# ScalarE fetches a second column of each step's fourth row pixel by pixel

## The chip, the core and the metric

The kernel runs on one core of one Trainium2 chip. A core has TensorE (PE; PEld is its weight load), VectorE (DVE), ScalarE (ACT), GpSimd (POOL) and SyncE (SP), each with a queue of instructions that it works through in order, and 16 DMA engines. SP, ACT and POOL can issue DMAs; "SPq" and "ACTq" in a row mark such an issue. Engines wait for one another through semaphores only. The metric is the device time of one execution in microseconds; of several runs the median counts.

## The reference

x is 4 images of 128 x 128 pixels with 64 channels. Four residual blocks are applied in turn, each on a group-normalised x:

```python
x = x + L0(gn(x))   # 3x3 convolution, then 1x1
x = x + L1(gn(x))   # deformable: 2 groups x 9 taps, each sampled at its own place
x = x + L2(gn(x))   # focal modulation: depthwise filters of 3, 5, 7 taps, Gelu, gates
x = x + L3(gn(x))   # triangle product per channel, layernorms, sigmoid gates
# L1, for each pixel, group and tap: place = grid + tap + offset, clipped to the image
out = wa * v[y0, x0] + wb * v[y1, x0] + wc * v[y0, x1] + wd * v[y1, x1]
```

L1 is what matters here: 18 columns (2 groups x 9 taps) of bilinear samples for each pixel, at places that the data decide. After it come a depthwise 3 x 3 and a 1 x 1 convolution.

## The kernel before

**Layout.** Two rows of an image lie side by side on the 128 partitions (64 channels each). For L1 a table in HBM (`table[b]`) holds, for each pixel of image b and each group, an entry with its four neighbours' channels, so one sample is one read of 512 bytes (128 floats).

**Steps.** L1 is computed in 128 steps, 32 for each image; a step does 4 rows (`ROWS`) of 128 pixels, row r into its own buffer `gat[r]`, which has 18 columns of 128 floats for each pixel (a pixel is a partition). For each row:
- POOL gathers a column for all 128 pixels with one indirect DMA (L573): 18 columns a row, but 17 in the fourth row (`gathered_by_pool`, L516), so 71 gathers a step. It waits for the row's indices (`idx_given`) and until the buffer has been summed in the step before (`summed`).
- The missing column (`FETCHED`, the fourth row's last) is fetched by SP, pixel by pixel (`fetch`, L785). SP waits for the places (`pixels_given`), brings them from a column over partitions (`pixel_at`) into one partition (`pixel_row`) with a DMA (L792), waits for that and for the buffer, and then, 16 pixels (`CHUNK`) at a time, loads the places into registers (L799) and issues 16 DMAs of 512 bytes (L804).
- DVE (`row`, L1731) waits for the gathers of the row (and of the fourth row also for the pixels), gives the next indices, multiplies the row by its bilinear weights (L1743) and sums four neighbours into `srow` (L1750). At the start of a step `indices` (L1677) computes places, weights and indices of the next step; its last part writes `pixel_at` once the DMA that reads the places before has landed (L1712).
- PE transposes `srow` into `pt` (L1354, L1358); ACT copies `pt` to `stt` in two copies a row: the first (L1068) and the second (L1072); PE multiplies by the folded weights (L1367) behind each copy.

**What is woven in.** The work of the other blocks stands in stages: for image 0's steps the first block and the tables of the images to come (`AHEAD`), for image b's steps the blocks L2 and L3 of image b - 1 (`BEHIND`): a norm step, 2 of context, 8 of depthwise, 4 of modulate, a norm step, 4 of operands, 2 of triangle, 4 of close, the rest plain, with nothing woven in. The work of the last image follows the 128 steps. For each engine the order is written out by hand: a step spans the times 0 to 14, each flow yields the time of its next piece, and `merged` and `weave` put the pieces in order of these times into the engine's one queue. A row's copies on ACT have the times 3r + 2 and 3r + 3. Between stages SP, ACT, PE and DVE meet (drain and wait for one another); POOL doesn't. In a depthwise step ACT issues the loads of context and bands at time 0 (L522, L526), and Gelu for the filters of 3, 5 and 7 taps (L955) stands at about 3.2, 6.5 and 9.7, each behind PE's filter (L1223). Ln and Exp of the layernorms are issued by `roots` (L966).

Of the kernel before, what the change touches and what calls it, by code (L numbers as in the profile page):

```python
# [23 lines left out]
I32 = mybir.dt.int32  # L24
# [5 lines left out]
ds = bass.ds  # L30
# [18 lines left out]
STEPS = NB * PER  # L49
FETCHED = (3, GK - 1)  # L50
CHUNK = 16
# [152 lines left out]
def build(nc, x, mats, vecs, conv_kt, conv_w, off_w, dw_w, pw_w, dw_b, gate_w, base_loc, base_idx, taps,  # L204
          out):
    ctx = ExitStack()
    with ctx:
        def sb(name, shape, dt=F32):
            return ctx.enter_context(nc.sbuf_tensor(name, shape, dt))
# [4 lines left out]
        def sems(*names):  # L214
            return tuple(ctx.enter_context(nc.semaphore(n)) for n in names)
# [54 lines left out]
        idx = sb("idx", [P, ROWS, GK], U32)  # L270
        pixel_at = sb("pixel_at", [P, 1], I32)
        pixel_row = sb("pixel_row", [1, P], I32)
        wtn = sb("wtn", [P, ROWS, GK, 4])
# [94 lines left out]
        with nc.Block() as block:  # L368
# [82 lines left out]
        turned_full, full_ready = sems("turned_full", "full_ready")  # L451
        pixels_given, pixel_row_in, pixels_in = composed, x_in[1], x_in[2]
        GIVEN0, ROW0, PIXELS0 = 2, 16, 16
        (padded_c,) = sems("padded_c")
# [10 lines left out]

        q_p, q_s, m_p, xo_s, m_cen_p, m_sq_s, m_var_p, m_lg_s, m_rs_s, m_y_s, m_o_p, m_added = sems(
            "q_p", "q_s", "m_p", "xo_s", "m_cen_p", "m_sq_s", "m_var_p", "m_lg_s", "m_rs_s", "m_y_s",
            "m_o_p", "m_added")
        ca_in = sems(*(f"ca_in{u}" for u in range(4)))

        t_cen_p, t_sq_s, t_var_p, t_lg_s, t_rs_s, t_y_s, ab_p, g_p, ab_s, g_s = sems(
            "t_cen_p", "t_sq_s", "t_var_p", "t_lg_s", "t_rs_s", "t_y_s", "ab_p", "g_p", "ab_s", "g_s")
        abg_out = sems(*(f"abg_out{u}" for u in range(4)))
# [3 lines left out]

        c_cen_p, c_sq_s, c_var_p, c_lg_s, c_rs_s, c_y_s, c_o_p, lin_s, res_s = sems(
            "c_cen_p", "c_sq_s", "c_var_p", "c_lg_s", "c_rs_s", "c_y_s", "c_o_p", "lin_s", "res_s")
        s_in, g_in, res_out = (sems(*(f"{n}{u}" for u in range(4))) for n in ("s_in", "g_in", "res_out"))  # L480
# [35 lines left out]
        def gathered_by_pool(r):  # L516

            return GK - 1 if r == FETCHED[0] else GK

# [19 lines left out]
        with nc.Block() as block:  # L539

            @block.gpsimd
            def _(pool):

                def shift_upper(t):
                    nc.gpsimd.tensor_scalar(xn[C:P, 4 * t + 1:4 * t + 5, 1:W + 1],
                                            xb[C:P, t * TILE:(t + 1) * TILE].rearrange("p (h w) -> p h w", w=W),
                                            gn[C:P, 0:1], gn[C:P, 1:2], ALU.mult, ALU.add).then_inc(upper, 1)

                pool.wait_ge(gn_done, 1)
                pool.wait_ge(padded, 1)  # L550
                for t in range(TB):
                    shift_upper(t)
                pool.wait_ge(upper, TB)
                for m in range(MCH):
                    for dy in range(3):
                        for dx in range(3):
                            nc.gpsimd.tensor_scalar(wk[:, m, dx, (3 - dy) * C:(4 - dy) * C], pw[:, m, 0:C],
                                                    dw[:, m, 3 * dy + dx:3 * dy + dx + 1], None, ALU.mult)\
                                .then_inc(wk_ready, 1)
                pool.wait_ge(wk_ready, N_ZERO + MCH * K9)  # L560
                pool.wait_ge(gn_done, 2)
                for t in range(TB):
                    shift_upper(t)
                pool.wait_ge(upper, 2 * TB)

                def step(n, b):
                    for r in range(ROWS):
                        v = n * ROWS + r
                        pool.wait_ge(idx_given, v + 1)  # L569
                        pool.wait_ge(summed, v + 1)  # L570
                        pool.sem_inc(started, 1)  # L571
                        for k in range(gathered_by_pool(r)):
# [11 lines left out]
            def _(sp):  # L584
# [200 lines left out]
                def fetch(n, b, at):  # L785

                    r, k = FETCHED
                    slot = k % K9 * G + k // K9
                    source = table[b].bitcast(U8)
                    yield at  # L790
                    sp.wait_ge(pixels_given, GIVEN0 + n + 1)
                    sp.dma_start(pixel_row[:], pixel_at[:]).then_inc(pixel_row_in, 16)  # L792
                    sp.wait_ge(pixel_row_in, ROW0 + 16 * n + 16)
                    sp.sem_inc(started, 1)
                    sp.wait_ge(summed, ROWS * n + r + 1)
                    sp.sem_inc(started, 1)
                    for first in range(0, P, CHUNK):
                        yield at + 4 * first / P
                        _, starts = nc.values_load_multi_w_load_instructions(  # L799
                            pixel_row[:, first:first + CHUNK], engines=[mybir.EngineType.SP], min_val=0,  # L800
                            max_val=4 * PAIR * (G * TABLE - 1),
                            skip_runtime_bounds_check_because="the coordinates are clipped to the image")
                        for p, start in enumerate(starts, first):
                            sp.dma_start(gat[r][p:p + 1, slot, :].bitcast(U8), source[ds(start, 4 * ENTRY)].unsqueeze(0))\  # L804
                                .then_inc(pixels_in, 16)

# [40 lines left out]
            def _(act):  # L847
# [117 lines left out]

                def roots(n, count, eps_, var_p, lg_s, y_s, rs_s):  # L966

                    for u in range(count + 1):
                        if u < count:
                            act.wait_ge(var_p, n(u) + 1 + count)  # L970
                            nc.scalar.activation(lg[u], banks[2 * u + 1], ACT.Ln, bias=eps_).then_inc(lg_s, 1)
                        if u:
                            act.wait_ge(lg_s, n(u - 1) + 1)
                            act.wait_ge(y_s, n(u - 1) + 1)
                            nc.scalar.activation(rs[u - 1], lg[u - 1], ACT.Exp, scale=-0.5).then_inc(rs_s, 1)
# [5 lines left out]
                def modulate(b, i):  # L981
# [11 lines left out]
                    yield 5  # L993
                    roots(n, flight(b), eps[:, 1:2], m_var_p, m_lg_s, m_y_s, m_rs_s)

                def operands(b, i):
# [7 lines left out]
                    ln_and_exp(b)  # L1004
                    roots(n, flight(b), eps[:, 0:1], t_var_p, t_lg_s, t_y_s, t_rs_s)
                    yield 7
# [29 lines left out]
                def close(b, i):  # L1036
# [12 lines left out]
                    yield 5  # L1049
                    roots(n, flight(b), eps[:, 0:1], c_var_p, c_lg_s, c_y_s, c_rs_s)  # L1050
                    yield 10
# [9 lines left out]
                def step(n, b, i):  # L1061

                    for r in range(ROWS):
# [12 lines left out]
                for a in (*gelu_s, ab_s, g_s, gate_s):  # L1076
                    act.sem_inc(a, 1)
                act.sem_inc(right_entries, 2)
                drive(act, meet, step, lambda: None, {"depthwise": depthwise_begin, "modulate": ln_and_exp, "close": ln_and_exp},
                      {"conv_norm": norm, "shift": shift, "conv_shift": lower_part, "table_norm": norm,  # L1080
# [348 lines left out]
            def _(dve):  # L1429
# [247 lines left out]
                def indices(n):  # L1677
# [27 lines left out]
                    for cx, wx in enumerate((w_lo, w_hi)):  # L1705
# [210 lines left out]
```

## Time and profile before

| | |
|---|---|
| median of 3 runs | 12193.87 us (12193.84 to 12196.55) |
| the profiled execution | 12192.18 us, its span 12190.4 us |
| granted TensorE clock, mean over the span | 0.776 |
| busy: POOL, PE, DVE, ACT | 71%, 63%, 42%, 15% |
| POOL's gathers | 9088 |
| SP's pixel DMAs | 16384 |

Times of a timeline count from the start of the span. "x128" behind a row means that 128 instructions of the kind follow each other; the number after the start is then the time from the first to the last. In square brackets stands how long the engine was idle before and what ended that.

### The profile page before, as it was taken

How to read it: one execution, taken by the hardware profiler on the slowest of the kernel's cores; microseconds unless marked ns; L12 is line 12 of the kernel's file. 1: busy time of each engine (PE TensorE's matmuls, PEld its weight loads, DVE VectorE, ACT ScalarE, POOL GpSimd, SP SyncE). 2: the span in 40 equal slices, each digit the busy share in tenths (PEclk: the TensorE clock that was granted, in tenths of full speed). 3: DMA queues.
4: the chain of work that ended last, by engine and by line, in shares of the span. 5: the costliest groups of instructions: out<-in, count | busy, mean ns of one | idle time of the engine just before them, and what ended most of it. 6: DMA issues, size and time to landing. Idle time of an engine off the chain costs nothing.

```text
span 12190.4 us, 137030 instructions
## 1 busy us (share of the span) xinstructions
PE 7646.7 (63%) x30934; PEld 5412.4 (44%) x30934; DVE 5177.5 (42%) x6121; ACT 1778.1 (15%) x2822; POOL 8661.5 (71%) x9172
## 2 busy tenths in 40 slices
PE   5676667666467765554457766555457765655488
PEld 3444444444346543333346644343335653333374
DVE  3344444434344443343345444344344544334333
ACT  1012111111011112110011111210001111211015
POOL 4777777777777777777777777777777777777700
PEclk8787778777678887776678877776678887877699
DMA  2333333433244423432234422342224532343272
GB/s 94 97 96 97 110 94 107 113 91 107 73 128 158 132 70 78 118 95 63 71 101 151 159 77 69 98 113 75 57 80 150 159 111 62 88 120 91 62 252 57
DMA packets 925529, 1256.69 MB, mean 103 GB/s; under 512 B 216152, under 2 KB 712216, under 8 KB 907096
## 3 DMA queue, kind: packets, MB, share of 16 engines
q0 software_dynamic: 290816, 596.17, 19.3%
q1 hardware_dynamic: 516904, 403.90, 11.0%
q10 hardware_dynamic: 117424, 252.73, 5.8%
q14 instruction: 296, 2.42, 0.1%
q8 instruction: 89, 1.46, 0.0%
HBM read 1069.42 MB, written 245.43 MB: 108 GB/s over the span
## 4 chain that ended last, share of the span: by engine, by line
POOL 69%; issue 23%; PE 4%; SPq 1%; DVE 1%; DMA 1%; POOLq 0%; ACT 0%; DVEq 0%; ACTq 0%; PEldq 0%
POOL gathered L573 69%; PE stage L1223 2%; PE stage L1095 1%; SPq L804 0%; PE acc L1095 0%; PE pt L1095 0%; PE acc L1367 0%; DMA room<-b_d 0%; POOLq L571 0%; SPq L799 0%; PE wtb L1095 0%; DMA gathered<-table,idx 0%; POOLq L579 0%; DVE srow L1750 0%; POOLq L569 0%
## 5 line engine op out<-in xcount | busy, mean ns | idle before, releaser
L573 POOL DMA_INDIRECT gathered<-table,idx x9088 | 8610.8, 947 | 2804.9 <-issue 2769.4
L1367 PE MATMUL acc<-stt,room 128*128 128x256 f32 (+2 forms) x15360 | 4151.2, 425 | 316.4 <-ACT stt L1068 316.4
L1367 PEld LDWEIGHTS acc<-stt,room 128*128 128x128 f32 (+1 forms) x15360 | 3148.3, 214 | 1236.4 <-issue 392.0
L1354 PE MATMUL pt<-mat,srow 128*128 128x128 f32 x2048 | 501.7, 391 | 3299.8 <-DVE srow L1750 3299.8
L1750 DVE TENSOR_REDUCE srow<-gathered 128x576 f32<-128x2304 f32 x512 | 2081.8, 4066 | 1.8
L1354 PEld LDWEIGHTS pt<-mat,srow 128*128 128x128 f32 x2048 | 326.3, 195 | 3557.5 <-DVE srow L1750 3536.6
L1719 DVE COPY idx<-idxn 128x18 uint32<-128x18 uint32 x512 | 99.2, 194 | 4253.4 <-DMA gathered<-table,idx 3885.9
L1068 ACT ACTIVATE stt<-pt 128x1024 f32<-128x1024 f32 (+1 forms) x512 | 415.4, 811 | 6631.6 <-PE pt L1354 6586.7
L1743 DVE TENSOR_TENSOR gathered<-gathered,wtb 128x2304 f32<-128x2304 f32 x512 | 1306.1, 2551 | 61.8 <-DMA gathered<-table,idx 61.2
L1095 PE MATMUL stage<-room,mat 128*128 128x512 f32 (+1 forms) x1360 | 791.0, 714 | 407.9 <-DMA room<-s_d 166.1
L1223 PEld LDWEIGHTS stage<-room 128*128 128x128 f32 x6784 | 826.5, 204 | 32.0 <-issue 29.5
L1223 PE MATMUL stage<-room 128*128 128x128 f32 x6784 | 828.3, 287 | 14.4 <-DMA room<-toep 11.1
L1095 PEld LDWEIGHTS stage<-room,mat 128*128 128x128 f32 x1360 | 296.6, 243 | 745.4 <-issue 457.9
L1162 PE MATMUL stage<-room,offw 128*72 (+1 forms) x768 | 378.9, 647 | 49.1 <-PEq L500 36.3
L1141 PE MATMUL stage<-room,cw 128*128 (+1 forms) x768 | 360.3, 625 | 39.5 <-PEq L500 36.4
L1694 DVE TENSOR_TENSOR loc<-off,base 128x144 f32<-128x144 f32 x128 | 39.4, 308 | 798.5 <-DMA off<-offs 789.4
L1072 ACT ACTIVATE stt<-pt 64x256 f32<-64x256 f32 (+1 forms) x512 | 166.2, 325 | 1428.4 <-PE pt L1358 1424.4
L1141 PEld LDWEIGHTS stage<-room,cw 128*128 128x128 f32 x768 | 150.5, 201 | 227.4 <-issue 226.5
L1162 PEld LDWEIGHTS stage<-room,offw 128*72 128x72 f32 x768 | 115.4, 158 | 270.2 <-issue 260.3
L1095 PE MATMUL stage<-room,scaled 128*128 x336 | 206.8, 715 | 15.5 <-SPq L500 6.8
L955 ACT ACTIVATE room<-stage 128x512 f32<-128x512 f32 x192 | 115.2, 600 | 686.8 <-PE stage L1223 686.5
L1358 PE MATMUL pt<-mat,srow 128*64 128x128 f32 x512 | 181.3, 354 | 1.1 <-ACT stt L1068 1.1
(213 smaller groups left out, 4159.8 us busy)
## 6 DMA issues: line engine op xcount, KB each, us to landing
gathered<-table SPq DMA_DIRECT2D x16384, 0.5 KB
gathered<-table,idx POOLq DMA_INDIRECT x9088
room<-toep ACTq DMA_DIRECT2D x48, 1792.0 KB, 10.0
room<-toep ACTq DMA_DIRECT2D x48, 1280.0 KB
room<-toep ACTq DMA_DIRECT2D x48, 768.0 KB, 8.2
table<-room SPq DMA_DIRECT2D x64, 512.0 KB, 3.1
toep<-in_taps SPq DMA_DIRECT2D x128, 224.0 KB
gathered<-toep SPq DMA_DIRECT2D x16, 1792.0 KB, 8.0
```

The costliest lines, as they stand in the source:

```text
L573: nc.gpsimd.indirect_dma_start(gat[r][:, k % K9 * G + k // K9, :], None, table[b].rearrange("(n e) -> n e", e=PAIR), bass.IndirectOffsetOn ...
L1068: nc.scalar.activation(stt[:, SLOT_OF[r], 0:4, 1:W + 1], over_slots(r, pt[:]), ACT.Copy)\
L1072: nc.scalar.activation(stt[0:C, SLOT_OF[r], 4, 1:W + 1], over_slots(r, pt[0:C, 0, :]), ACT.Copy)\
L1095: return nc.tensor.matmul(dst, w, r, start=True, stop=True)
L1141: ins = nc.tensor.matmul(PB[u][:], cw0[:, 2 * k:2 * k + 2, :].rearrange("p a c -> p (a c)"), window(k // 3, k % 3, t), start=(k == 0), sto ...
L1162: ins = nc.tensor.matmul(PB[0][0:2 * NOFF, :], offw[:, k, :], window(k // 3, k % 3, t), start=(k == 0), stop=(k == 5))
L1223: ins = nc.tensor.matmul(PB[2 * u + l % 2][:, c * W:(c + 1) * W], band(b, l, u)[:, c * k + dx, :], cin[l][u][:, c, at:at + W], start=(dx = ...
L1354: ins = nc.tensor.transpose(pt[:, m, :], srow[r % 2][:, m * P:(m + 1) * P], M["ident"])
L1358: nc.tensor.transpose(pt[0:C, 0, :], srow[r % 2][:, (MCH - 1) * P:KC], M["ident"])\
L1367: ins = nc.tensor.matmul(sums_of[:, pairs, :], wk[0:kk, m, dx, at:at + P], stt[0:kk, slots, m, dx:dx + W], start=start and m == 0 and dx == 0,
L1743: tt(g4, g4, wb, ALU.mult).then_inc(weighted, 1)
L1750: nc.vector.tensor_reduce(srow[r % 2][:].rearrange("p (s c) -> p s c", c=CG), gat[r][:].rearrange("p s (q c) -> p s c q", q=4), AX.X, ALU. ...
```

## The change

ACT fetches one more column of the fourth row (`BY_ACT` = 8, the last tap of the first group) in the same way as SP fetches column 17 (`BY_SP`); POOL gathers 16 columns of the fourth row. `pixel_at`, `pixel_row` and the three semaphores exist twice now. ACT asks for the places and waits at time 0.5 of a step, and its eight pieces of 16 pixels stand at the times listed below, all ahead of the fourth row's copies (11 and 12). To have semaphores left, the three that Ln signals are made one (`lg_s`), with counts adjusted.

```diff
-FETCHED = (3, GK - 1)
+FETCHED_ROW = ROWS - 1
+BY_SP, BY_ACT = GK - 1, K9 - 1
...
         def gathered_by_pool(r):
-            return GK - 1 if r == FETCHED[0] else GK
+            return [k for k in range(GK) if r != FETCHED_ROW or k not in (BY_SP, BY_ACT)]
...
+        def fetch_pixels(eng, engine, b, k, first):
+            slot = k % K9 * G + k // K9
+            _, starts = nc.values_load_multi_w_load_instructions(
+                pixel_row[k][:, first:first + CHUNK], engines=[engine], min_val=0, max_val=4 * PAIR * (G * TABLE - 1),
+                skip_runtime_bounds_check_because="the coordinates are clipped to the image")
+            for p, start in enumerate(starts, first):
+                eng.dma_start(gat[FETCHED_ROW][p:p + 1, slot, :].bitcast(U8),
+                              table[b].bitcast(U8)[ds(start, 4 * ENTRY)].unsqueeze(0)).then_inc(pixels_in[k], 16)
...
+                def fetch(n, b):
+                    k = BY_ACT
+                    yield 0.5
+                    act.wait_ge(pixels_given[k], GIVEN0[k] + n + 1)
+                    act.dma_start(pixel_row[k][:], pixel_at[k][:]).then_inc(pixel_row_in[k], 16)
+                    act.wait_ge(pixel_row_in[k], ROW0[k] + 16 * n + 16)
+                    act.sem_inc(started, 1)
+                    act.wait_ge(summed, ROWS * n + FETCHED_ROW + 1)
+                    act.sem_inc(started, 1)
+                    for q, at in enumerate((0.6, 1, 1.5, 3.3, 4, 6.3, 7, 9.3)):
+                        yield at
+                        fetch_pixels(act, mybir.EngineType.Activation, b, k, q * CHUNK)
+
                 def step(n, b, i):
+                    return merged(copies(n), fetch(n, b))
...
-                    dve.wait_ge(pixel_row_in, ROW0 + 16 * n)
-                    ts(pixel_at[:], entry[:, FETCHED[0], FETCHED[1]:FETCHED[1] + 1], 4.0 * PAIR,
-                       4.0 * PAIR * TABLE * (FETCHED[1] // K9), ALU.mult, ALU.add).then_inc(pixels_given, 1)
+                    for k in (BY_SP, BY_ACT):
+                        dve.wait_ge(pixel_row_in[k], ROW0[k] + 16 * n)
+                        ts(pixel_at[k][:], entry[:, FETCHED_ROW, k:k + 1], 4.0 * PAIR, 4.0 * PAIR * TABLE * (k // K9),
+                           ALU.mult, ALU.add).then_inc(pixels_given[k], 1)
...
-                    dve.wait_ge(landed[r], 16 * gathered_by_pool(r) * (n + 1))
-                    if r == FETCHED[0]:
-                        dve.wait_ge(pixels_in, PIXELS0 + 16 * P * (n + 1))
+                    dve.wait_ge(landed[r], 16 * len(gathered_by_pool(r)) * (n + 1))
+                    for k in (BY_SP, BY_ACT) if r == FETCHED_ROW else ():
+                        dve.wait_ge(pixels_in[k], PIXELS0[k] + 16 * P * (n + 1))
```

## Rows read from the trace of the kernel before

**Rows 1.** The page, part 1: busy time of each engine, share of the span, instructions.

```profile
PE 7646.7 (63%) x30934; PEld 5412.4 (44%) x30934; DVE 5177.5 (42%) x6121; ACT 1778.1 (15%) x2822; POOL 8661.5 (71%) x9172
```

**Rows 2.** The page, part 4: the chain that ended last, shares of the span by engine.

```profile
POOL 69%; issue 23%; PE 4%; SPq 1%; DVE 1%; DMA 1%; POOLq 0%; ACT 0%; DVEq 0%; ACTq 0%; PEldq 0%
```

**Rows 3.** The page, part 5: the group of POOL's gathers (busy, mean ns | idle before, releaser).

```profile
L573 POOL DMA_INDIRECT gathered<-table,idx x9088 | 8610.8, 947 | 2804.9 <-issue 2769.4
```

**Rows 4.** Timeline of POOL: first gathers of steps 40, 41 and 95 (start, us, engine, line).

```profile
3731.08 0.95 POOL L573 DMA_INDIRECT gathered<-table,idx  x1 [0.30 <-issue]
...
3820.87 0.94 POOL L573 DMA_INDIRECT gathered<-table,idx  x1 [0.30 <-issue]
...
8627.31 0.94 POOL L573 DMA_INDIRECT gathered<-table,idx  x1 [0.30 <-issue]
```

**Rows 5.** Timeline of SP, step 49: places asked for, pixels fetched.

```profile
4560.55 0.58 SPq L792 DMA_DIRECT2D pixel_row<-pixel_at  x1
4563.94 51.31 SPq L804 DMA_DIRECT2D gathered<-table  x128
```

**Rows 6.** Timeline of ACT, the plain step 94.

```profile
8552.42 0.38 ACT L1072 ACTIVATE stt<-pt 64x256 f32<-64x256 f32 x1 [3.23 <-PE pt L1358]
8570.53 1.03 ACT L1068 ACTIVATE stt<-pt 128x1024 f32<-128x1024 f32 x1 [17.74 <-PE pt L1354]
8574.78 0.38 ACT L1072 ACTIVATE stt<-pt 64x256 f32<-64x256 f32 x1 [3.22 <-PE pt L1358]
...
8641.04 0.38 ACT L1072 ACTIVATE stt<-pt 64x256 f32<-64x256 f32 x1 [3.23 <-PE pt L1358]
```

**Rows 7.** Timeline of DVE, step 94: multiply of the fourth row.

```profile
8628.80 2.56 DVE L1743 TENSOR_TENSOR gathered<-gathered,wtb 128x2304 f32<-128x2304 f32 x1
```

**Rows 8.** Timeline of ACT, a depthwise step (40).

```profile
3754.88 0.38 ACT L1072 ACTIVATE stt<-pt 64x256 f32<-64x256 f32 x1 [3.10 <-PE pt L1358]
...
3758.41 0.40 ACTq L526 DMA_DIRECT2D room<-toep  x1
3758.98 1.28 ACT L1068 ACT_TABLE_LOAD   x1 [3.72 <-issue]
3768.30 1.03 ACT L1068 ACTIVATE stt<-pt 128x1024 f32<-128x1024 f32 x1 [8.04 <-PE pt L1354]
...
3779.90 0.60 ACT L955 ACTIVATE room<-stage 128x512 f32<-128x512 f32 x1 [0.79 <-PE stage L1223]
3785.35 0.60 ACT L1068 ACTIVATE stt<-pt 128x512 f32<-128x512 f32 x1 [4.86 <-PE pt L1354]
...
3797.25 0.60 ACT L955 ACTIVATE room<-stage 128x512 f32<-128x512 f32 x1 [3.87 <-PE stage L1223]
3815.78 0.60 ACT L1068 ACTIVATE stt<-pt 128x512 f32<-128x512 f32 x1 [17.93 <-PE pt L1354]
...
3844.16 0.38 ACT L1072 ACTIVATE stt<-pt 64x256 f32<-64x256 f32 x1 [3.10 <-PE pt L1358]
```

**Rows 9.** Timeline of DVE, step 40, before the third row's sum and that sum.

```profile
3807.62 0.68 DVE L1596 TENSOR_TENSOR room<-room 128x512 f32<-128x512 f32 x1
...
3810.52 4.05 DVE L1750 TENSOR_REDUCE srow<-gathered 128x576 f32<-128x2304 f32 x1
```

**Rows 10.** Timeline of SP, step 34: a 4096 KB load ahead of the places.

```profile
3216.84 0.43 SPq L586 DMA_DIRECT2D room<-x  x1
3217.31 0.50 SPq L792 DMA_DIRECT2D pixel_row<-pixel_at  x1
3232.82 51.35 SPq L804 DMA_DIRECT2D gathered<-table  x128
```

**Rows 11.** The page, part 6: a band load of 768 KB, us from issue to landing.

```profile
room<-toep ACTq DMA_DIRECT2D x48, 768.0 KB, 8.2
```

**Rows 12.** Timeline of ACT, triangle step 54: row two's first copy, row four's second.

```profile
5071.28 0.60 ACT L1068 ACTIVATE stt<-pt 128x512 f32<-128x512 f32 x1 [40.87 <-issue]
...
5096.28 0.38 ACT L1072 ACTIVATE stt<-pt 64x256 f32<-64x256 f32 x1 [2.90 <-PE pt L1358]
```

More of the change, by code:

```diff
@@ L270, in build @@
         idx = sb("idx", [P, ROWS, GK], U32)
-        pixel_at = sb("pixel_at", [P, 1], I32)
-        pixel_row = sb("pixel_row", [1, P], I32)
+        pixel_at = {k: sb(f"pixel_at{k}", [P, 1], I32) for k in (BY_SP, BY_ACT)}
+        pixel_row = {k: sb(f"pixel_row{k}", [1, P], I32) for k in (BY_SP, BY_ACT)}
         wtn = sb("wtn", [P, ROWS, GK, 4])
@@ L451, in build @@
         turned_full, full_ready = sems("turned_full", "full_ready")
-        pixels_given, pixel_row_in, pixels_in = composed, x_in[1], x_in[2]
-        GIVEN0, ROW0, PIXELS0 = 2, 16, 16
+        act_given, act_row_in = sems("act_given", "act_row_in")
+        pixels_given = {BY_SP: composed, BY_ACT: act_given}
+        pixel_row_in = {BY_SP: x_in[1], BY_ACT: act_row_in}
+        pixels_in = {BY_SP: x_in[2], BY_ACT: loaded}
+        GIVEN0 = {BY_SP: 2, BY_ACT: 0}
+        ROW0 = {BY_SP: 16, BY_ACT: 16}
+        PIXELS0 = {BY_SP: 16, BY_ACT: 16 * N_LOAD}
         (padded_c,) = sems("padded_c")
@@ L571, in step @@
                         pool.sem_inc(started, 1)
-                        for k in range(gathered_by_pool(r)):
+                        for k in gathered_by_pool(r):
                             nc.gpsimd.indirect_dma_start(
@@ L785, in fetch @@
                 def fetch(n, b, at):
-                    r, k = FETCHED
-                    slot = k % K9 * G + k // K9
-                    source = table[b].bitcast(U8)
+                    k = BY_SP
                     yield at
-                    sp.wait_ge(pixels_given, GIVEN0 + n + 1)
-                    sp.dma_start(pixel_row[:], pixel_at[:]).then_inc(pixel_row_in, 16)
-                    sp.wait_ge(pixel_row_in, ROW0 + 16 * n + 16)
+                    sp.wait_ge(pixels_given[k], GIVEN0[k] + n + 1)
+                    sp.dma_start(pixel_row[k][:], pixel_at[k][:]).then_inc(pixel_row_in[k], 16)
+                    sp.wait_ge(pixel_row_in[k], ROW0[k] + 16 * n + 16)
                     sp.sem_inc(started, 1)
-                    sp.wait_ge(summed, ROWS * n + r + 1)
+                    sp.wait_ge(summed, ROWS * n + FETCHED_ROW + 1)
                     sp.sem_inc(started, 1)
@@ L798, in fetch @@
                         yield at + 4 * first / P
[L799 to L805, printed above, removed]
+                        fetch_pixels(sp, mybir.EngineType.SP, b, k, first)
                 def step(n, b, i):
@@ L964, in depthwise, with roots @@
                         act.dma_start(group(mixd, b, 2 * i + u), mix[u]).then_inc(mix_out[u], 16)
-                def roots(n, count, eps_, var_p, lg_s, y_s, rs_s):
+                def roots(n, count, eps_, var_p, y_s, rs_s, before):
                     for u in range(count + 1):
@@ L972, in roots @@
                         if u:
-                            act.wait_ge(lg_s, n(u - 1) + 1)
+                            act.wait_ge(lg_s, n(u - 1) + before + 1)
                             act.wait_ge(y_s, n(u - 1) + 1)
@@ L1059, in over_slots, with copies @@
                     return a.unsqueeze(1).to_broadcast([a.shape[0], len(range(at.start, at.stop, at.step or 1)), *a.shape[1:]])
+                def fetch(n, b):
[10 more added lines that the diff above has]
+                        fetch_pixels(act, mybir.EngineType.Activation, b, k, q * CHUNK)
                 def step(n, b, i):
+                    return merged(copies(n), fetch(n, b))
+                def copies(n):
                     for r in range(ROWS):
@@ L1078, in _ @@
                 act.sem_inc(right_entries, 2)
+                act.sem_inc(pixel_row_in[BY_ACT], 16)
                 drive(act, meet, step, lambda: None, {"depthwise": depthwise_begin, "modulate": ln_and_exp, "close": ln_and_exp},
```

18 lines of the change are left out of this document (9 added, 9 removed).

## Prediction, written before the result

> **What bounds the kernel now.** I read the busy table first [rows 1]: GpSimd (POOL) is busy 71% of the span, ScalarE (ACT) 15%. The chain that ended last then gives POOL's gathers 69% and "issue", the gap between gathers, 23% [rows 2]. The group of those gathers shows 8610.8 us busy and 2769.4 us of issue gap for 9088 of them, so (8610.8 + 2769.4) / 9088 = 1.252 us each, and of 2804.9 us idle only 35 are not issue gaps [rows 3]. So POOL runs through all 128 steps without waiting, 71 gathers a step: 88.9 us. In the depthwise stage a step takes 71 gathers and 3820.87 - 3731.08 = 89.8 us [rows 4]. Everything else lives in POOL's shadow, and the question is whether it still does.
>
> **What is removed.** One gather a step: 128 x 1.252 = 160 us of POOL. A step becomes 70 x 1.252 = 87.6 us, if nothing else comes late. In the 24 depthwise steps POOL's extra 0.9 us would go too if it is no longer pressed: 21 us.
>
> **What is added, and its price.** SP already fetches one column: 128 DMAs with a register load ahead of each 16, 51.3 us from the first DMA to the last [rows 5]. The eight pieces are 6.5 us each with their register load. ACT has no rows of such pixels; its own DMA issues take 0.39 to 0.53 us [rows 8], the size of SP's loads, so I give ACT SP's price. As ends: half of it (26 us, nothing in the rows speaks for it) and the 0.53 us of its dearest issue per pixel (68 us). ACT also issues the DMA of the row of places and waits for it: 3.4 us from its issue to the first pixel, on an empty queue [rows 5]. DVE gets one more operation on one column beside a wait (below); POOL's gathers hide it. The shared semaphore for Ln costs nothing: same instructions, same order.
>
> That ACT is idle 85% doesn't decide, since its queue is in order. Behind each piece stand the copies that PE waits for, and Gelu, Ln, Exp and Sigmoid of the woven stage. The closed loop: fourth row's second copy of step n-1, places, three pieces, copies of row one, two pieces, row two, two pieces, row three, one piece, landing, multiply of row four, its copies. I call it ACT's round and add it up with all gathered data there.
>
> **Plain step** [rows 6, 7]. First pixel at 3.6; three pieces end at 22. Row one's two copies end 4.6 later (8574.78 + 0.38 - 8570.53), 26.7; two pieces 39.7; row two 44; two pieces 57; row three 61; one piece 67.5, landing of the last about 1.5 us behind its issue: 68.5. The multiply of row four to the end of its second copy is 8641.42 - 8628.80 = 12.6. Round 81 us, under 87.6: here the fetch is hidden, and the loop regains about 7 us a step when it is late.
>
> **Depthwise step** [rows 8, 9]. Time 0 is 3755.26, the end of the fourth row's second copy. The loads of context and bands are issued until 3758.8, at 3.6. The request for the places stands behind them in ACT's queue. What this costs SP shows: behind one 4096 KB load its first pixel came 15.5 us after the request (3232.82 - 3217.31) [rows 10], against 3.4 without. Here 2 x 256 and 2 x 768 KB are ahead, and a 768 KB band lands 8.2 us after its issue [rows 11], so the places are there at about 11.5 and the first pixel at 13. Three pieces: 31.5. Table load and first copy: 33.8. To the second Gelu of the 3-tap filter 3779.90 - 3769.33 = 10.6: 44.4. Two pieces and row two's copy: 58.0. To the second Gelu of the 5-tap filter 3797.25 - 3785.95 = 11.3, and its 0.6: 69.9 (a piece lies beside PE here). DVE's four operations 2.9, reduce 4.05, turn and copy 1.8: 78.7 (second piece hidden). From row three's copy to the fourth row's second copy 3844.54 - 3816.38 = 28.2, beside which the last piece lies: 106.9. The same sum without pieces is some 80, which fits the 89.8 set by POOL. Round 107, 19.4 over POOL's 87.6, in 8 steps of each of images 1 to 3: 155 us an image. Without the queueing behind the loads it is 99, and 11.6 x 8 = 93.
>
> The Trainium skill (DMA: Bandwidth & Descriptors, "Queues, rings and completion order") says that descriptors of one ring are consumed in order and that a completion is written only after earlier writes of that DMA engine. By that rule the places wait for the loads: the 107. Were ACT's request independent, it would be the 99. The trace's 15.5 against 3.4 us agrees with the rule on SP's queue; no row has it on ACT's.
>
> **The other stages** (estimates by the same walk). Triangle: in step 54, row two's first copy comes only at 5071.28, as it waits for loads that SP issues behind its own fetch, and the fourth row's second copy ends at 5096.66, 25.4 later [rows 12]; three pieces (19.5 us) fall into just that stretch, where every copy follows the one before, and the round was already about POOL's: 21 x 2 = 42 an image. Operands: ACT's own work and two table changes make the round about 92.5: 5 x 4 = 20. Context and the norms 25, the first modulate step 12 (the rest 88, nothing), close 22; their start behind a meeting is in this. Some 118 an image, halfway between a plain and a depthwise round; its ends are 60 and 200. For image 0 (shift puts ACT work at the end of a norm step, table into the four after) I take 20 net of what the loop can lend, ends 0 and 120.
>
> **What can be lent.** POOL is only held once DVE's sum of a row is later than POOL's next gather into it. For row four that is 3 x 18 x 1.252 = 67.6 us into the next step, and a sum ends 1.2 us ahead of the first copy (3815.78 - 3814.57), which with the 4.6 to the end of the second is 5.8: the second copy may end 73 us into the step [rows 6, 8, 9]. Now it is 3755.26 - 3731.08 = 24 in depthwise and 8641.42 - 8627.31 = 14 in plain steps [rows 4, 6, 8]. So some 59 us are lent once, at the first image; later only what six plain steps give back, 6 x 7 = 42. I count it: images 1 to 3 lose 155 + 118 - 42 = 231 each, 693; image 1 comes in with 15 us instead of 42 as image 0 has used the rest: 27; image 0 20; the last step's loop ends 30 us later behind POOL, and the work after it starts that much later. 770 us together.
>
> **A wait that is added** and easily missed: DVE's indices of the next step wait for the places' DMA of this step (L1712). SP issued it early, ACT only after the fourth row's copies. Behind it on DVE stands row one's multiply; in depthwise it starts at 13, when the places are there, and its copy is due at 33, so it costs nothing more; POOL's first gather of the step after needs that row, which the 73 us limit covers within 5 us.
>
> **Sum.** 12190.4 - 160 - 21 + 770 = 12779 us of span, +1.8 around it (12192.2 profiled) 12781; the median of the runs is 12193.9, so 12,780 us, 4.8% slower.
>
> **Rivals.** (A) The gain stands: all pieces fall into waits of ACT and the lent 59 us carry the rest: 12194 - 160 = 12,033. For it: ACT idle 85%, plain steps fit, and in the trace most idle time of ACT is ahead of a row's first copy. Against: the depthwise sum, where the pieces stand between a copy and PE's next filter. 0.11. (B) The loop is lent more and costs less: no queueing behind the loads (99), other stages at 60: (93 + 60 - 42) x 3 = 333, +50: 12194 - 181 + 383 = 12,396. 0.22. (C) Both fetches slow each other, as SP and ACT together then send twice as many pixels in the same time; 4 us more in some 80 rounds: 13,100. 0.10. The trace has only SP's stream; POOL's gathers beside it show no slowing. (D) The change leaves POOL as it was or the pieces go out with less than half of SP's price: 12,030 to 12,200. 0.02. The forecast has 0.55.
>
> **Chances and range.** A measurement here can tell about 0.2% (24 us) from no change. Faster by over that: A and most of D, 0.12. Within: 0.02, where the loss happens to meet 181 us. Slower: 0.86. Range 12,330 to 13,120: it takes in B and C, leaves out A and the tails; the forecast's own range is 12,560 to 13,000.
>
> **What would show it.** Right: POOL's gathers gain idle time ended by DVE's reduce or index copy, a thousand us less the gain, most of it in the last depthwise steps and after them to the close stage; depthwise steps near 107 us from the fourth or so on, plain ones at 81 to 88; 8960 gathers; ACT's first copy of row one at 33 us after the round's start instead of 13 (3768.30 - 3755.26). Wrong: POOL idle still only issue gaps; a pixel piece on ACT far from 6.5 us; the places landing at 6 us in depthwise steps; or triangle and close steps unchanged at 88.

## The result, and the profile after

The changed kernel takes 13,126.3 us (median of 4 runs, 13,121.4 to 13,127.0); the kernel before took 12,194.0 us beside it. The ratio is 1.0764, 95% interval 1.0751 to 1.0778: 7.6% slower. The forecast was 12,780, slower by 4.8%; the time lies 6 us above the range. Direction and mechanism held, the size did not: +932 us instead of +586.

Busy time of the engines in the changed kernel, as in [rows 1]:

```profile
PE 7747.5 (59%) x30934; PEld 5476.9 (42%) x30934; DVE 5179.3 (39%) x6249; ACT 1764.3 (13%) x2822; POOL 8540.1 (65%) x9044
```

POOL works 121 us less, and DVE and ScalarE as long as before within 14 us. PE is busy 101 us longer with the same 30934 matmuls, at a mean granted clock of 0.761 against 0.776. ScalarE's wait for PE's turned rows ahead of a second copy is 3.23 us in a plain round, as before. ScalarE's pixels don't appear, as issuing DMAs is not counted as busy. The group of POOL's gathers, against [rows 3] (busy, mean ns, idle time before, and what ended it):

```profile
L589 POOL DMA_INDIRECT gathered<-table,idx x8960 | 8489.5, 947 | 3829.2 <-issue 3331.3 <-DVE idx L1746 342.1 <-DVE srow L1777 155.9
```

There are 128 gathers fewer, each as long as before. Issue gaps alone would be 8960 x 0.305 = 2730 us, so of its 3829.2 us idle POOL now waits some 1100 us. The timeline of POOL shows where: at the first gather of step 40, and at the first one of that step's third row:

```profile
3813.28 0.94 POOL L589 DMA_INDIRECT gathered<-table,idx  x1 [8.21 <-DVE idx L1746]
...
3873.02 0.94 POOL L589 DMA_INDIRECT gathered<-table,idx  x1 [14.83 <-issue]
```

The second wait is put down to "issue" though it is a wait as well: POOL waits for the sum and the indices of a row of the step before. Elsewhere the gap is 0.30.

ScalarE in a depthwise round (image 1; [rows 8] show it before). A line "x48" is three pieces of 16 pixels, L963 is Gelu:

```profile
3901.34 0.38 ACT L1097 ACTIVATE stt<-pt 64x256 f32<-64x256 f32 x1 [3.06 <-PE pt L1384]
3901.48 1.03 ACTq L972 DMA_DIRECT2D mixd<-room  x2
3905.93 0.42 ACTq L538 DMA_DIRECT2D room<-ctxd  x1
...
3908.38 0.57 ACTq L1074 DMA_DIRECT2D pixel_row<-pixel_at  x1
3918.59 18.59 ACTq L533 DMA_DIRECT2D gathered<-table  x48
...
3938.63 1.03 ACT L1093 ACTIVATE stt<-pt 128x1024 f32<-128x1024 f32 x1
...
3951.42 12.46 ACTq L533 DMA_DIRECT2D gathered<-table  x32
3964.04 0.60 ACT L1093 ACTIVATE stt<-pt 128x512 f32<-128x512 f32 x1 [13.32 <-issue]
...
3969.24 5.34 ACTq L533 DMA_DIRECT2D gathered<-table  x16
...
3975.24 0.60 ACT L963 ACTIVATE room<-stage 128x512 f32<-128x512 f32 x1 [7.03 <-issue]
...
3978.20 0.60 ACT L963 ACTIVATE room<-stage 128x512 f32<-128x512 f32 x1 [2.36 <-PE stage L1249]
...
4013.65 0.38 ACT L1097 ACTIVATE stt<-pt 64x256 f32<-64x256 f32 x1 [3.10 <-PE pt L1384]
```

Read it from the top. The round starts when the first line ends (3901.72). The request for the places goes out behind the loads at 3908.38, and the first pixel only at 3918.59, 16.9 us into the round (13 predicted). The first copy comes at 36.9 (33 predicted), and the round ends at 4014.03: 112.3 us. Two things are to be seen. Between the stores at 3901.48 (1.03 long) and the first load at 3905.93 lie 3.4 us in which ScalarE issues nothing and waits for no semaphore. They follow the branch back, the jump to the start of its loop over steps. And 10.2 us pass from request to first pixel. The same place in image 3:

```profile
10171.44 0.38 ACT L1097 ACTIVATE stt<-pt 64x256 f32<-64x256 f32 x1 [3.10 <-PE pt L1384]
10171.58 1.01 ACTq L972 DMA_DIRECT2D mixd<-room  x2
10173.19 0.41 ACTq L538 DMA_DIRECT2D room<-ctxd  x1
```

Here the gap is 0.6 us, and the rounds of image 3 are 109.5 against 111.7 and 112.5 in images 1 and 2.

What goes on in the gap is seen in part 3 of the page, in the queue that it calls "instruction" (packets, MB, share), first before, then changed:

```profile
q14 instruction: 296, 2.42, 0.1%
q14 instruction: 632, 5.18, 0.1%
```

In the window 3902.6 to 4014.8, the round of image 1, that queue moves five packets of 8 KB for all engines together, one of them in the window 3902.6 to 3905.6, inside the gap:

```profile
q14 instruction: 5, 0.04, 0.1%
```

In the window 10172.7 to 10281.9, the same round of image 3, the view has no such line.

DVE in the same round of image 1. Before it may multiply it waits until ScalarE's places have landed (the wait of L1739, which the prediction calls L1712 in the old numbering):

```profile
3917.05 0.15 DVE L1740 TENSOR_SCALAR pixel_at<-loc 128x1 int32<-128x1 f32 x1 [10.60 <-DMA pixel_row<-pixel_at]
```

A plain round (step 94, as [rows 6]): 9236.99 - 9154.73 = 82.3 us, predicted 81, with 3.8 to 4.1 us from the request to the first pixel:

```profile
9154.35 0.38 ACT L1097 ACTIVATE stt<-pt 64x256 f32<-64x256 f32 x1 [3.23 <-PE pt L1384]
...
9236.61 0.38 ACT L1097 ACTIVATE stt<-pt 64x256 f32<-64x256 f32 x1 [3.23 <-PE pt L1384]
9237.01 0.48 ACTq L1074 DMA_DIRECT2D pixel_row<-pixel_at  x1
9241.12 18.77 ACTq L533 DMA_DIRECT2D gathered<-table  x48
```

In the first triangle step SP and ScalarE follow each other. SP's pixels, and its next load behind them:

```profile
5313.86 44.80 SPq L533 DMA_DIRECT2D gathered<-table  x112
5358.95 0.43 SPq L749 DMA_DIRECT2D room<-a_d  x1
```

ScalarE in the same step, row two's first copy and the piece behind it, as [rows 12]:

```profile
5367.66 0.60 ACT L1093 ACTIVATE stt<-pt 128x512 f32<-128x512 f32 x1 [37.12 <-PE pt L1380]
...
5372.80 5.24 ACTq L533 DMA_DIRECT2D gathered<-table  x16
```

SP's pixels hold SP's loads back as before, and three of ScalarE's pieces come behind the copy at 5367.66. The round ends at 5414.2, 46.6 us from that copy, where it was 25.4: 21.2 us more, for three pieces that the prediction put at 19.5.

The mean round by stage over images 1 to 3, in us, each between the ends of the fourth row's second copies (L1097). The columns e2, e4 and e10 are experiments told below:

| stage | before | predicted | changed | e2 | e4 | e10 |
|---|---|---|---|---|---|---|
| norms, context (4 rounds) | 89.0 | 93.9 | 92.7 | 90.6 | 90.5 | 89.2 |
| depthwise (8) | 90.8 | 107.0 | 111.2 | 103.2 | 107.6 | 93.3 |
| modulate (4) | 87.0 | 90.6 | 93.7 | 92.2 | 92.2 | 82.0 |
| operands (4) | 89.7 | 92.6 | 95.0 | 92.1 | 93.6 | 89.7 |
| triangle (2) | 91.9 | 108.6 | 114.3 | 114.5 | 113.9 | 105.1 |
| close (4) | 86.4 | 93.1 | 97.8 | 95.4 | 95.4 | 84.4 |
| plain (6) | 88.3 | 80.6 | 82.2 | 80.3 | 81.8 | 85.0 |

"Predicted" is 87.6 plus the stage's share of the loss in the prediction. Before, the rounds lie around POOL's 88.9, which sets their mean. Now their mean over an image is 97.2 to 98.3, and POOL's 87.5 sets it no longer.

### The profile page after: what moved, and what is told of

Its sections match the earlier page's. It is cut to its first block and busy times, and to the rows that moved or that the text cites. A ratio compares the mean times of both kernels' runs of the same rounds, so it can differ in the third digit from the quotient of the medians.

```text
span 13125.0 us, 171671 instructions
## 1 busy us (share of the span) xinstructions
PE 7747.5 (59%) x30934; PEld 5476.9 (42%) x30934; DVE 5179.3 (39%) x6249; ACT 1764.3 (13%) x2822; POOL 8540.1 (65%) x9044
## 5 line engine op out<-in xcount | busy, mean ns | idle before, releaser
L589 POOL DMA_INDIRECT gathered<-table,idx x8960 | 8489.5, 947 | 3829.2 <-issue 3331.3
L1393 PE MATMUL acc<-stt,room 128*128 128x256 f32 (+2 forms) x15360 | 4296.3, 435 | 2140.3 <-ACT stt L1093 2133.1
L1393 PEld LDWEIGHTS acc<-stt,room 128*128 128x128 f32 (+1 forms) x15360 | 3237.6, 221 | 3098.1 <-ACT stt L1093 1829.3
L1380 PE MATMUL pt<-mat,srow 128*128 128x128 f32 x2048 | 433.8, 349 | 2235.0 <-DVE srow L1777 2235.0
L1380 PEld LDWEIGHTS pt<-mat,srow 128*128 128x128 f32 x2048 | 289.8, 175 | 2466.0 <-DVE srow L1777 2389.4
L1121 PE MATMUL stage<-room,mat 128*128 128x512 f32 (+1 forms) x1360 | 815.7, 733 | 427.1 <-ACT room L1056 133.3
L1756 DVE SCALAR_TENSOR_TENSOR xs<-acc,fused,xr 128x256 f32<-128x256 f32 x128 | 61.4, 480 | 1272.3 <-PE acc L1393 1230.0
L1097 ACT ACTIVATE stt<-pt 64x256 f32<-64x256 f32 (+1 forms) x512 | 166.2, 325 | 1426.2 <-PE pt L1384 1421.2
L1622 DVE TENSOR_TENSOR room<-room 128x512 f32<-128x512 f32 x128 | 88.2, 689 | 458.1 <-ACT room L963 457.9
L963 ACT ACTIVATE room<-stage 128x512 f32<-128x512 f32 x192 | 115.0, 600 | 687.0 <-PE stage L1249 510.7
```

Of the source, the lines that this page charges most:

```text
L589: nc.gpsimd.indirect_dma_start(gat[r][:, k % K9 * G + k // K9, :], None, table[b].rearrange("(n e) -> n e", e=PAIR), bass.IndirectOffsetOn ...
L963: nc.scalar.activation(dst, PB[2 * u + l % 2][:].rearrange("p (c w) -> p c w", w=W), ACT.Gelu).then_inc(gelu_s[u], 1)
L1097: nc.scalar.activation(stt[0:C, SLOT_OF[r], 4, 1:W + 1], over_slots(r, pt[0:C, 0, :]), ACT.Copy)\
L1121: return nc.tensor.matmul(dst, w, r, start=True, stop=True)
L1380: ins = nc.tensor.transpose(pt[:, m, :], srow[r % 2][:, m * P:(m + 1) * P], M["ident"])
L1393: ins = nc.tensor.matmul(sums_of[:, pairs, :], wk[0:kk, m, dx, at:at + P], stt[0:kk, slots, m, dx:dx + W], start=start and m == 0 and dx == 0,
```

## Experiments

All twelve are timed against the kernel before, whose medians beside them were 12,192.6 to 12,213.6 us.

**e1: what POOL gains.** ScalarE's fetch is left out and POOL doesn't gather the column either, so the multiply reads zeros there.

```diff
-                    return merged(copies(n), fetch(n, b))
+                    return copies(n)
...
-                    for k in (BY_SP, BY_ACT) if r == FETCHED_ROW else ():
+                    for k in (BY_SP,) if r == FETCHED_ROW else ():
...
+                    nc.vector.memset(gat[FETCHED_ROW][:, BY_ACT % K9 * G + BY_ACT // K9, :], 0.0).then_inc(act_given, 1)
```

> This kernel leaves the second fetched column out altogether: POOL gathers 16 columns of the fourth row, ScalarE fetches nothing, and the multiply reads zeros there. It prices POOL's side alone. If POOL's 70 gathers (70 x 1.25 = 87.5 us) set every step again: 12,194 - 128 x 1.252 = 12,034 us, steps at 87.5 us, idle of POOL only issue gaps. Rival, POOL was not the bound before (then what ScalarE took away is more than the fetch): above 12,120 us.

12,030.8 us, ratio 0.9867 (0.9850 to 0.9883). The gain alone is what the prediction put it at, 160 us. POOL's waits are issue gaps again:

```profile
L589 POOL DMA_INDIRECT gathered<-table,idx x8960 | 8484.7, 947 | 2766.0 <-issue 2727.4 <-DVE idx L1746 38.5
```

So the fetch itself costs 13,126 - 12,031 = 1,095 us, of which the forecast held 12,780 - 12,034 = 746.

**e5: whether the gain counts.** POOL gathers all 71 columns, ScalarE fetches into a spare tile.

```diff
-            return [k for k in range(GK) if r != FETCHED_ROW or k not in (BY_SP, BY_ACT)]
+            return [k for k in range(GK) if r != FETCHED_ROW or k != BY_SP]
...
+                into = spare[p:p + 1, :] if k == BY_ACT else gat[FETCHED_ROW][p:p + 1, slot, :]
```

> POOL gathers all the columns it gathered before (71 a step) and ScalarE still fetches its pixels, into a spare tile, with the same waits. So the cost is there and the gain is not. Theory (from image 0 on ScalarE's round is the bound and POOL only follows): the saved gather is worth nothing, 13,126 to 13,160 us. Rival (cost and gain add up): 13,126 + 160 = 13,286 us.

13,125.1 us, ratio 1.0745 (1.0727 to 1.0763): the time of the changed kernel to within 1 us. The kernel before took 12,213.6 us beside it, so by the ratios it is some 20 us less; the rival wanted 160 more. Its gathers take 120 us more, and POOL waits that much less:

```profile
L591 POOL DMA_INDIRECT gathered<-table,idx x9088 | 8609.6, 947 | 3711.7 <-issue 3355.2 <-DVE idx L1748 223.4 <-DVE srow L1779 133.1
```

The rival, that cost and gain add up, is out. Where ScalarE's round sets the time, the gathers saved are worth nothing.

**e3: depthwise alone.** No pixels in the 24 woven depthwise steps.

```diff
-                    return merged(copies(n), fetch(n, b))
+                    return merged(copies(n), credit(n) if in_depthwise[0] else fetch(n, b))
...
+                    act.sem_inc(pixels_in[k], 16 * P)
```

> ScalarE fetches no pixel in the 24 woven depthwise steps (the column keeps what it had; the semaphore is credited by hand), everything else as changed. Theory: these rounds fall under POOL's 87.5 us, which gives 24 x (111.2 - 87.5) = 570 us back and refills what can be lent before modulate to close: about 12,480 us (12,400 to 12,560). Rival (each step loses alike, 1092 / 128 = 8.5 us): 13,126 - 24 x 8.5 = 12,920 us.

12,491.2 us, ratio 1.0245 (1.0228 to 1.0262), 11 us from the theory. Depthwise rounds fall to 85.9 us. The rival, that each step loses alike, is out: without the fetch in these 24 steps 635 us come back of the 1,095 that the whole fetch costs.

**e11: triangle and close alone.** As e3, for these 18 steps.

> ScalarE fetches no pixel in the 18 woven triangle and close steps (the column keeps what it had; the semaphore is credited by hand). Theory (ScalarE's pieces behind SP's fetch are the whole excess of these rounds): triangle falls from 114.6 to 92, close from 98 to 87, 18 rounds give 3 x (45 + 45) = 270 us: 12,855 us (12,820 to 12,890). Rival (SP's own fetch makes them, ScalarE's pieces lie beside it): triangle stays over 105, 100 us or less: above 13,020 us.

12,817.0 us, ratio 1.0515 (1.0499 to 1.0531): 309 us back, somewhat more than the theory's 270. Triangle rounds fall from 114.3 to 91.5, close from 97.8 to 84.8. SP's fetch was in the triangle round before; with ScalarE's pieces the round is 23 us longer than without. If the two add up (they were not tried together), depthwise, triangle and close hold 635 + 309 = 944 of the fetch's 1,095 us.

**e2: the places asked for early.** Moved between the two copies of the fourth row of the step before.

```diff
-                    act.wait_ge(pixels_given[k], GIVEN0[k] + n + 1)
-                    act.dma_start(pixel_row[k][:], pixel_at[k][:]).then_inc(pixel_row_in[k], 16)
                     act.wait_ge(pixel_row_in[k], ROW0[k] + 16 * n + 16)
...
+                        yield 11.5
+                        ask_places(n + 1)
...
+                def ask_places(n):
+                    k = BY_ACT
+                    act.wait_ge(pixels_given[k], GIVEN0[k] + n + 1)
+                    act.dma_start(pixel_row[k][:], pixel_at[k][:]).then_inc(pixel_row_in[k], 16)
```

> ScalarE asks for the row of places of the next step between the fourth row's two copies, ahead of the depthwise loads, and doesn't wait behind them. Theory (each depthwise round holds the queueing behind the band loads): the first pixel comes 7 to 8 us after the round's start instead of 16.9, depthwise rounds fall from 109-112 to about 102 us, the others by 3 us: 24 x 9.5 + 80 x 3 = 470 us at most, some of it lost where POOL's 87.5 us is the bound: 12,650 to 12,800 us. Rival (the places' wait is hidden, DVE's chain of multiplies sets the round): no more than 60 us off the changed kernel, above 13,060 us.

12,749.0 us, ratio 1.0459 (1.0442 to 1.0477): 377 us better, in the range of the theory. The depthwise round, image 1:

```profile
3806.07 0.51 ACTq L1087 DMA_DIRECT2D pixel_row<-pixel_at  x1
...
3810.24 0.38 ACT L1103 ACTIVATE stt<-pt 64x256 f32<-64x256 f32 x1 [3.10 <-PE pt L1390]
3810.39 1.02 ACTq L972 DMA_DIRECT2D mixd<-room  x2
3815.00 0.41 ACTq L538 DMA_DIRECT2D room<-ctxd  x1
...
3818.88 17.25 ACTq L533 DMA_DIRECT2D gathered<-table  x42
```

The first pixel comes 3818.88 - 3810.62 = 8.3 us into the round instead of 16.9, and depthwise rounds are 8.0 us shorter. So the 8 us that the prediction put on queueing behind the loads were right. The Trainium skill (DMA: Bandwidth & Descriptors, "Queues, rings and completion order") has descriptors of one ring consumed in order; the trace of the changed kernel agrees on ScalarE's queue too: the places landed 8.6 us after their request, 0.3 us after the second band load ahead of them.

**e4: the gap at the branch.** ScalarE's loops over steps written out.

```diff
+            if flat:
+                for j in range(stage.steps):
+                    round_(j)
```

> Same work in the same order, but ScalarE's loops over the steps of a stage are written out, so that it has no branch back. In the changed kernel 44 of its branches back are followed by 2.4 to 4.8 us in which it issues nothing (141.7 us together), in the kernel before none of 66. Theory (these gaps belong to the branch and lie on the round): about 12,985 us, depthwise rounds of images 1 and 2 at 109 like those of image 3. Rival (the instructions have to come from memory anyway, and the gap appears elsewhere in the straight code): 13,126 us within 30.

12,932.9 us, ratio 1.0606 (1.0588 to 1.0623): 193 us better, 52 more than the gaps add up to (141.7). The edit did a second thing I had not foreseen: written out, the kernel has 87 activation table loads of 1.28 us where it had 149, and both loads of a depthwise round are gone:

```profile
3879.84 0.38 ACT L1103 ACTIVATE stt<-pt 64x256 f32<-64x256 f32 x1 [3.05 <-PE pt L1390]
3879.85 0.99 ACTq L978 DMA_DIRECT2D mixd<-room  x2
3880.88 0.57 ACTq L544 DMA_DIRECT2D room<-ctxd  x1
...
3893.97 19.08 ACTq L539 DMA_DIRECT2D gathered<-table  x48
3913.16 1.03 ACT L1099 ACTIVATE stt<-pt 128x1024 f32<-128x1024 f32 x1 [32.94 <-issue]
```

So e4 doesn't price the gap cleanly. Image 3 separates the two: it had no gap in depthwise, and its round still fell from 109.5 to 107.4, which is the table loads. Images 1 and 2 fell by 4.2 and 4.7, and the difference of some 2.3 is what the gap costs a round. The rival (straight code has the gap too) is out: there is none after the stores.

**e6, e7, e8: pieces moved to SP.** Of the second column SP fetches two (e6, e7) or three (e8) pieces, with early places; e7 and e8 with loops written out.

```diff
...
+                    sp.wait_ge(pixel_row_in[BY_ACT], ROW0[BY_ACT] + 16 * n + 16)
+                    for q in range(BY_SP_TOO):
+                        fetch_pixels(sp, mybir.EngineType.SP, b, BY_ACT, q * CHUNK)
```

> Places asked for early as in e2, and of the second column's eight pieces SP fetches two (ten in all) and ScalarE six. Theory: two pieces of 6.6 us leave each of ScalarE's rounds: depthwise 105 - 13 = 92 (88 in image 3), all rounds but triangle's (115, where SP's fetch is in the round, now 13 us longer, while ScalarE's part is 13 us shorter) under 87.5; excess over POOL some 90 us an image, of which about 55 can be lent and given back: 12,034 + 50 + 3 x 40 = 12,200 us (12,120 to 12,300), about the kernel before. Rival (SP's ten pieces, 64 us with the 3.4 us for the places and its loads behind them, become the round in every stage): above 12,350 us.

12,925.7 us, ratio 1.0583 (1.0565 to 1.0600): the rival held, I was wrong by 700 us. SP's rounds follow the same arithmetic as ScalarE's. Its ten pieces take 63.8 us, its own waits and loads lie around them (modulate, image 1):

```profile
4741.15 3.21 SPq L721 DMA_DIRECT2D room<-mixd  x4
...
4754.70 0.57 SPq L807 DMA_DIRECT2D pixel_row<-pixel_at  x1
4759.15 63.81 SPq L534 DMA_DIRECT2D gathered<-table  x160
```

Depthwise is at 95.0, but operands at 100.8, norms and context at 97, and image 0 takes 3,090.6 us for its rounds 1 to 31 instead of 2,843.8. I had summed ScalarE's round only. (The 2,843.8 are those of the changed kernel.)

> e6 with ScalarE's loops over steps written out as in e4. Theory: the gap of 3 us at each branch back goes, depthwise rounds at 88: 60 to 100 us less than e6, 12,080 to 12,180 us, just under the kernel before. Rival (with two pieces less the body is short enough and there is no gap to remove, or POOL is the bound anyway): as e6 within 20 us.

12,908.3 us, ratio 1.0568 (1.0551 to 1.0586), 17 us from e6: its rival held. What ScalarE's loops cost is mostly hidden here; in e6 four of its branches have a gap, 13 us together.

> As e7, but SP fetches three of the eight pieces and ScalarE five. Theory for depthwise as the bound: rounds fall to 82, under POOL's 87.5: 20 to 40 us less than e7, 12,060 to 12,140 us. Rival (SP's eleven pieces, 71 us, now make triangle and close rounds 6 us longer and leave SP too little room for bands and tables of image 0): slower than e7 by 20 us or more.

13,642.5 us, ratio 1.1169 (1.1150 to 1.1188): its rival held. One piece more on SP costs 734 us, 5.7 a step, though ScalarE has one less.

**e9, e10: fewer pieces, the rest by POOL.** Early places; POOL gathers rows 0 to 63 (e9) or 0 to 31 (e10) of the column.

```diff
+                            rows = FROM if r == FETCHED_ROW and k == BY_ACT else P
-                                gat[r][:, k % K9 * G + k // K9, :], None, table[b].rearrange("(n e) -> n e", e=PAIR),
-                                bass.IndirectOffsetOnAxis(ap=idx[:, r, k:k + 1], axis=0))\
+                                gat[r][0:rows, k % K9 * G + k // K9, :], None, table[b].rearrange("(n e) -> n e", e=PAIR),
+                                bass.IndirectOffsetOnAxis(ap=idx[0:rows, r, k:k + 1], axis=0))\
```

> Places asked for early; of the second column ScalarE fetches rows 64 to 127 in four pieces and POOL gathers rows 0 to 63 in one gather of half the partitions. Theory: four pieces (26.5 us) leave each round of e2, so depthwise is at 77, triangle at 88 and POOL the bound again; then the time is 12,034 + 128 x (period of a 64-row gather, which no run has shown: 0.63 us if it goes by rows, 1.25 if it is fixed): 12,114 to 12,194 us, and slower than before by nothing. Rival (the loop is still over 87.5 in triangle and close by more than can be lent): 12,250 us or more.

12,192.5 us, ratio 0.9999 (0.9990 to 1.0008).

> As e9, with POOL gathering rows 0 to 31 of the column and ScalarE six pieces. Theory: two pieces less than e2: depthwise 105 - 13 = 92 less the 3 us gap of the branch, which e6 with as short a body didn't have: 89; triangle 101, close 86: some 40 us an image over POOL, which can be lent: 12,034 + 30 + 128 x (0.31 to 1.25): 12,100 to 12,230 us. Rival (rounds add up and nothing is lent back): 12,300 us or more.

12,188.1 us, ratio 0.9996 (0.9987 to 1.0005). Both are no different from the kernel before, at the upper end of the first range and inside the second. The fetch is hidden, and nothing is gained, since a gather of few rows costs nearly as much as a whole one. Three of POOL's gathers in e10, the middle one of 32 rows:

```profile
3805.72 0.94 POOL L592 DMA_INDIRECT gathered<-table,idx  x1 [0.30 <-issue]
3806.97 0.86 POOL L592 DMA_INDIRECT gathered<-table,idx  x1 [0.30 <-issue]
3808.13 0.96 POOL L592 DMA_INDIRECT gathered<-table,idx  x1 [0.31 <-issue]
```

**e12: the same without that gather** (its 32 rows keep zeros). Against e10:

```diff
-            return [k for k in range(GK) if r != FETCHED_ROW or k != BY_SP]
+            return [k for k in range(GK) if r != FETCHED_ROW or k not in (BY_SP, BY_ACT)]
```

> e10 without POOL's gather of 32 rows (those rows of the column keep zeros): what six pieces, asked for early, would give if the other two cost nobody anything. Theory (six pieces are hidden even at 87.5 us a step, only triangle and depthwise above it, which is lent): 12,034 to 12,060 us. Rival (e10 is at the limit; the loop sets the time as soon as POOL is faster): 12,100 us or more.

12,040.1 us, ratio 0.9873 (0.9856 to 0.9889). Six pieces with early places are all but free even at POOL's faster pace (e1: 12,030.8). Eight cost 709 us more (e2: 12,749.0). No version here that computes the whole beats the kernel before by more than the noise.

## Why the prediction was wrong in size

**Held.** The gain of one gather a step: -160 predicted, e1 shows -162. That ScalarE's queue, not its busy time, decides, and that the gain is worthless then: e5. Queueing behind the loads: e2. The last step: the second copy of the fourth row ends 133.3 us behind POOL's start, against 102.3, so 31 us later where 30 were predicted. The work after it takes 613 us in both. POOL's new idle time in images 1 to 3 lies from depthwise to close, as said. Rival C (the two streams slow each other) is out: SP's piece takes 6.54 us on average in both traces, and in the changed kernel ScalarE's takes 6.66 us where SP issues pixels all the while (612 of them) and 6.78 where SP issues none (257). The further 21 us of POOL in depthwise e1 doesn't show: its depthwise steps still take 88.2 us against 87.4 elsewhere.

**Failed: the sum of the rounds, "images 1 to 3 lose 155 + 118 - 42 = 231 each".** The first term is depthwise, the second the other woven stages, the third what plain steps give back. From the table the three measured 189, 169 and 32 us on average: 189 + 169 - 32 = 326. By image the rounds exceed 87.6 us by 325, 343 and 308 us. That is 283 us of the 346 missed, and 63 lie in image 0 (its last round ends at 3126.7; the forecast implies 12,779 - 613 - 3 x (32 x 87.6 + 231) = 3063). Over the three images the shortfall is 102 us in depthwise, 57 in close, 37 in modulate, 34 in triangle, 29 in operands and 28 in plain rounds; context and norms were 14 too dear. (These add up to 273, as the prediction's stages add up to 121 an image and not to its 118.) Of the 95 us missed an image, 34 lie in depthwise, 51 in the other woven stages, which the prediction put in "by the same walk" without writing the walk out, and 10 in plain steps.

Depthwise was written out, and its marks can be laid on the trace. Means of the 24 rounds, in us:

| from, to | predicted | changed |
|---|---|---|
| round's start, request for the places | 3.6 | 6.4 |
| request, first pixel | 9.4 | 9.9 |
| three pieces | 18.5 | 18.9 |
| table load, row one's first copy | 2.3 | 2.5 |
| to the second Gelu of 3 taps | 10.6 | 10.0 |
| that Gelu, two pieces, row two's first copy | 13.6 | 14.5 |
| to the end of the second Gelu of 5 taps, a piece between | 11.9 | 13.9 |
| to the end of row three's first copy | 8.8 | 7.0 |
| to the end of the round | 28.2 | 28.2 |
| round | 106.9 | 111.2 |

Three steps of the working are seen in it.

- "The loads of context and bands are issued until 3758.8, at 3.6": the branch back was a term that was missing. In the changed kernel 44 of ScalarE's branches back are followed by 2.4 to 4.8 us without an instruction, 141.7 us together, of which 46 us in depthwise (in 14 of the 24 rounds), 68 in the other stages of images 1 to 3 and 27.5 in image 0. Of the 2.8 us that the request comes late on average they are 1.9. The first round of the stage has none, as it follows a meeting of the engines, and image 3's depthwise has none, where the request comes at 3.7. In the kernel before no branch of ScalarE is followed by more than 0.8 us. The trace of before could have told me: SP, whose loops already held 128 pixels, had 21 such gaps of 3.6 us on average.
- "The eight pieces are 6.5 us each ... I give ACT SP's price": ScalarE's takes 6.72 us from register load to last issue (mean of 1024). In a depthwise round, where five pieces lie open, three and two of them took 0.4 and 0.9 us more than summed. The plain round, which has no gap and about seven open pieces (7 x 0.22 = 1.5), was missed by 1.6.
- "(a piece lies beside PE here)": the piece between row two's copies and the Gelu of 5 taps is not beside PE. It holds back the first Gelu (3975.24 in the round shown, "issue"), and the second then waits for PE again: 2.0 us. The next line was summed 1.8 too dear and hides it.

At full length the gaps make 114 us of the 283 in images 1 to 3 and 27.5 of the 63 in image 0; by e4 a depthwise round gets 2.3 of their 3.3 us back. e4 as a whole, which takes away the gaps and 62 table loads, gives 193 us. How the rest divides is an account from the trace that no run isolates. In close (57 short, 26 of it gaps) and triangle (34 short, 5 of it gaps) most stays open; e11 prices these two stages, not the reason. So does the rest of image 0.

**Rival A** (all pieces hidden, 12,033) names what e12 reaches with two pieces fewer and the places ahead of the loads. It was wrong for this kernel but not by much in design: two pieces and one queue position lie between e12's 12,040 (which leaves 32 rows of the column out) and 13,126. **Rival B** (no queueing behind the loads) is e2 but for the size: 12,749, not 12,396. B also put the other stages at 60 us an image, where 169 were measured.

## What to carry to other kernels

An engine that is idle most of the time can still be the bound. Sum its queue from one event to the same one a step later, everything in it at its price, DMA issues and register loads included. Write this sum out for every stage, and do it for each engine whose queue grows: e6 failed for SP just as this change does for ScalarE. The gain of one engine is real only up to the round of the next, and what a round has beyond that is paid in full. Ask for small things that others wait for ahead of large loads on the same queue. And when a loop's body grows, look behind its branch back for time in which the engine does nothing.

## What the runs showed of the hardware that I had not expected

- **A branch back can cost 3 us, and instructions are fetched in that time.** With no pixel in its loops ScalarE has no such gap, with 64 pixels a step none (e9), with 96 four (e6 and e10), with 128 forty-four; SP has 21 with 128 and 64 with 160 (e6). So it comes with the body's length. In each of the 44 gaps, and in each of SP's, an 8 KB packet of the queue that the page calls "instruction" starts, and ScalarE's next instruction follows 1.5 to 2.1 us after the last of them; of ScalarE's 206 other branches 13 have one in the 3.3 us behind them.
- **Length isn't all.** Image 3's depthwise loop holds 128 pixels and has no gap in the changed kernel and in e2. In e11, where only later stages differ, it has gaps of 3.1 to 3.5 us, and its rounds are 111.1 against 109.5. Its whole round needs no instruction packet in the changed kernel and five in e11. That points to where the code lies in memory, but no run changes the place alone.
- **An indirect gather hardly depends on its rows.** From one to the next: 1.249 us for 128 rows, 1.208 for 64 and 1.172 for 32 (medians of 128).
- **Straight code has fewer activation table loads** than the same code in a loop: 87 against 149 (e4).
